# Block attention with routed tokens, heavy half: another order of the steps on TensorE and ScalarE

## The reference

```python
light_out = light_local_attn(x, ...)      # windows of 128 tokens, 8 heads of 64
scores_q, idx_q = route(x, q_routing_token, 256)     # 256 of the tokens as queries
scores_kv, idx_kv = route(x, kv_routing_token, 512)  # all 512 tokens as keys
routed_out = heavy_attn(routed_q, routed_kv, scores_kv, ...)
heavy_out = zeros.at[idx_q].set(routed_out * scores_q)
return light_out + heavy_out
```

```python
q = (rmsnorm(xq) @ wq)          # 256 queries, 8 heads of 64
k, v = (rmsnorm(context) @ wkv) # 512 keys, 8 heads of 64
out = softmax(q k^T) v @ wo
```

## Time and profile before

| | us |
|---|---|
| median of three runs | 2500.14 |
| the profiled execution, its own time | 2494.2 |
| its span | 2492.2 |
| PE busy in the span | 2329.9 (93%) |
| DVE / ACT / POOL busy | 1410.5 / 950.6 / 613.6 |
| heavy half (first scores of step 0 to the last product with values) | 575.96 to 974.6 |

### The profile page before, as it was taken

The page is one execution under the profiler, slowest core; times in us unless marked ns, Lnnn a source line. Parts: engine busy times, 40 slices in busy tenths (PEclk is TensorE's granted clock), DMA queues, the critical chain, the costliest instruction groups (busy, mean ns, idle before and its releaser), DMA issues.

```text
span 2492.2 us, 40543 instructions
## 1 busy us (share of the span) xinstructions
PE 2329.9 (93%) x15438; PEld 1656.4 (66%) x15438; DVE 1410.5 (57%) x2881; ACT 950.6 (38%) x2288; POOL 613.6 (25%) x548
## 2 busy tenths in 40 slices
PE   6997999999999998998999999988984999999998
PEld 4444677776666665444666665544553999999997
DVE  7886654674544555887466533348885444444442
ACT  1366655444444543332233322124653222222222
POOL 3234222252001002211233100014455122222222
PEclk8998999999999999999999999989996999999999
DMA  5011211121001000100001029502126222222221
GB/s 202 1 35 51 91 35 52 52 83 54 26 26 52 26 26 26 71 1 18 1 1 36 1 95 326 185 0 110 40 80 244 58 36 37 35 36 36 36 35 26
DMA packets 72087, 148.36 MB, mean 60 GB/s; under 512 B 11704, under 2 KB 59065, under 8 KB 69441
## 3 DMA queue, kind: packets, MB, share of 16 engines
q1 hardware_dynamic: 39600, 104.61, 12.3%
q0 software_dynamic: 16368, 26.23, 5.4%
q10 hardware_dynamic: 15936, 15.03, 2.1%
HBM read 107.42 MB, written 74.76 MB: 73 GB/s over the span
## 4 chain that ended last, share of the span: by engine, by line
PE 81%; DVE 10%; ACT 4%; issue 2%; POOL 2%; DMA 1%; SPq 0%; DVEq 0%; POOLq 0%; ACTq 0%
PE PS L2366 14%; PE PS L2392 7%; PE PS L2822 5%; PE PS L2834 5%; PE PS L1540 4%; PE PS L1531 4%; PE PS L2050 3%; PE PS L2062 3%; PE PS L2891 3%; PE PS L602 3%; PE PS L2882 3%; PE PS L2856 3%; DVE mem L1148 2%; DVE mem L1143 2%; PE PS L2927 2%
## 5 line engine op out<-in xcount | busy, mean ns | idle before, releaser
L2366 PEld LDWEIGHTS PS<-ctx2T,x_all 128*128 128x128 f32 x3124 | 361.2, 193 | 10.1 <-DVE x_all L2515 6.5
L2366 PE MATMUL PS<-ctx2T,x_all 128*128 128x128 f32 x3124 | 361.8, 276 | 5.9 <-DVE x_all L2515 5.1
L2563 POOL DMA_INDIRECT out_x<-xnT,moe_small x71 | 130.9, 1843 | 427.7 <-ACT xnT L2448 424.7
L2392 PE MATMUL PS<-mem,moe_small 128*128 x852 | 195.8, 379 | 0.8 <-ACT xnT L2448 0.8
L2515 DVE COPY x_all<-mem 128x2816 f32 x71 | 115.5, 1627 | 109.6 <-issue 96.9
L2392 PEld LDWEIGHTS PS<-mem,moe_small 128*128 128x128 f32 x852 | 156.4, 190 | 19.4 <-issue 1.2
L1148 DVE RECIPROCAL mem<-PS 128x512 f32<-128x512 f32 x48 | 160.9, 3351 | 11.3 <-PE PS L671 11.0
L1143 DVE TENSOR_REDUCE mem<-PS 128x32 f32<-128x2048 f32 x48 | 109.9, 2289 | 50.8 <-PE PS L627 50.7
L3208 DVE TENSOR_REDUCE moe_small<-PS 128x2 f32<-128x1024 f32 x64 | 78.5, 1226 | 99.2 <-PE PS L2882 99.2
L3353 POOL TENSOR_TENSOR mem<-mem,moe_small 128x512 f32<-128x512 f32 x64 | 82.2, 1304 | 207.5 <-DVE moe_small L3218 207.4
L3032 ACT ACTIVATE mem<-PS,moe_small 128x128 f32<-128x128 f32 x256 | 89.9, 377 | 94.2 <-DVE moe_small L3203 94.2
(11 more groups left out here) (382 smaller groups left out, 4596.9 us busy)
## 6 DMA issues: line engine op xcount, KB each, us to landing
slots<-in_trash_rows SPq DMA_DIRECT2D x8, 4290.0 KB, 63.8
mem<-in_L_ffn_experts SPq DMA_DIRECT2D x8, 2176.0 KB, 13.6
xn<-slots ACTq DMA_DIRECT2D x53, 130.0 KB, 2.1
x_all<-in_x SPq DMA_DIRECT2D x8, 512.0 KB, 8.1
xn<-unit_rows SPq DMA_DIRECT2D x8, 512.0 KB, 4.5
mem<-unit_rows SPq DMA_DIRECT2D x8, 512.0 KB, 4.3
out_x<-x_all ACTq DMA_DIRECT2D x8, 512.0 KB, 2.9
unit_rows<-moe_small SPq DMA_DIRECT2D x7, 512.0 KB, 3.2
```

Of the source, the lines that this page charges most:

```text
L2366: last = nc.tensor.matmul(PS[:, moe_bank(j, part), c * P:(c + 1) * P], m.w[:, j % 2, k, at:at + P], m.rowT[:, j % 2, k, :], start=k == 0, ...
L2392: last = nc.tensor.matmul(PS[:, MOE_BANK_Y, 0:D], m.hT[:, j % 2, n, :], w[:, :, at:at + D], start=n == 0, stop=n == KE - 1)
L2563: nc.gpsimd.indirect_dma_start(s.T["out"], bass.IndirectOffsetOnAxis(s.token[:, j % 4:j % 4 + 1], 0), m.result[:, j % 4, :], None, compute ...
```

## The change

The change only moves calls. On PE, `heavy_values(u - 1)` at the end of step u becomes `heavy_values(u - 2)` directly behind the scores of step u (`light_values` of the last two light steps likewise), and the last one falls into a step 65. In odd steps `queries` moves in front of `turn_probs`. `turn_routed` moves from the odd step into the even step in front of it, to its end. ACT is put in the matching order: in odd steps it first copies the finished pair of products (`copy_heavy_oT`, before in the even step), then the queries, then does the exponentials, then copies the two turned halves; before, it copied the halves, did the exponentials and then copied the queries. DVE and POOL are unchanged, and no instruction is added or removed.

```diff
--- before.py
+++ after.py
@@ -2970,22 +2970,20 @@
         nxt = u // QT + 1
         if u < HEAVY_STEPS:
             heavy_scores(u)
-        if u == 0:
-            light_values(LIGHT_STEPS - 2)
+        if u < 2:
+            light_values(LIGHT_STEPS - 2 + u)
+        elif u <= HEAVY_STEPS + 1:
+            heavy_values(u - 2)
         if u % QT == 0 and nxt < LIGHT_STEPS:
             keys(heavy, nxt)
-        if u % QT == 1 and nxt < LIGHT_STEPS and nxt % CT == 0:
-            turn_routed(nxt // CT)
+        if u % QT == 1 and nxt < LIGHT_STEPS:
+            queries(heavy, nxt)
         if u <= HEAVY_STEPS:
             turn_probs(*((heavy, u - 1) if u else (light, LIGHT_STEPS - 1)))
         if u % QT == 0 and nxt < LIGHT_STEPS:
             values_of_tokens(heavy, nxt)
-        if u % QT == 1 and nxt < LIGHT_STEPS:
-            queries(heavy, nxt)
-        if u == 0:
-            light_values(LIGHT_STEPS - 1)
-        elif u <= HEAVY_STEPS:
-            heavy_values(u - 1)
+            if nxt % CT == 0:
+                turn_routed(nxt // CT)
         if LIGHT_STEPS + u - Y_LATER < NT:
             light_out(LIGHT_STEPS + u - Y_LATER)
         i, qt = (u - 2 * CT - 1) // (2 * CT), (u - 2 * CT - 1) % (2 * CT)
@@ -3092,25 +3090,23 @@
             nc.scalar.activation(s.e_min[0:B, :], s.e[0:B, :], ACT.Exp).then_inc(s.sems["score_row"], 1)
     for u in range(HEAVY_STEPS + 3):
         nxt = u // QT + 1
-        if u % QT == 1 and nxt < LIGHT_STEPS and nxt % CT == 0:
-            copy_routed(nxt // CT)
+        if u % QT == 1 and 2 <= u <= HEAVY_STEPS + 1:
+            copy_heavy_oT(u // QT - 1)
+        if u % QT == 1 and nxt < LIGHT_STEPS:
+            copy_queries(heavy, nxt)
+        if u < HEAVY_STEPS:
+            heavy_exponentials(u)
+        if u < 2:
+            copy_light_oT(LIGHT_STEPS - 2 + u)
         if u % QT == 1 and u <= HEAVY_STEPS:
             copy_probs(heavy, u - 1, 0)
             copy_probs(heavy, u - 1, 1)
-        if u < HEAVY_STEPS:
-            heavy_exponentials(u)
-        if u == 0:
-            copy_light_oT(LIGHT_STEPS - 2)
         if u % QT == 0 and u <= HEAVY_STEPS:
             copy_probs(*((heavy, u - 1) if u else (light, LIGHT_STEPS - 1)), 0)
         if u % QT == 0 and nxt < LIGHT_STEPS:
             copy_values(heavy, nxt)
-        if u % QT == 1 and nxt < LIGHT_STEPS:
-            copy_queries(heavy, nxt)
-        if u == 0:
-            copy_light_oT(LIGHT_STEPS - 1)
-        elif u <= HEAVY_STEPS and u % QT == 0:
-            copy_heavy_oT(u // QT - 1)
+            if nxt % CT == 0:
+                copy_routed(nxt // CT)
         i, qt = (u - 2 * CT - 1) // (2 * CT), (u - 2 * CT - 1) % (2 * CT)
         if u > 2 * CT and qt < QT:
             act.wait_ge(heavy.sems["y_psum"], QT * i + qt + 1)
```

## The result

The changed kernel takes 2513.2 us (median of 19 runs, 2505.77 to 2515.88), the kernel before 2503.39 us (19 runs, 2499.08 to 2506.93). The ratio is 1.0034, with a 95% interval from 1.0026 to 1.0042: slower by 0.34%, between 6.5 and 10.5 us, where 7.8 had been worked out. In itself the median lies 5.3 us above the 2507.9 of the forecast; 3.3 of these are its base, since the three runs it started from had a median of 2500.14 and the 19 have 2503.39.

A forecast was written before the change was run, and what follows sets the result against it. TensorE, busy 373.6 of 384 us between 576 and 960, was taken as the bound. Odd steps +9.9, start -1.0 and +1.5, end -2.6 gave +7.8; 2500.1 + 7.8 = 2507.9 us, range 2497 to 2514.

The forecast's parts named there:

- The odd step: Heavy odd steps with queries, without output product: exponentials wait for the queries' copy, 0.45 longer each, 22 times, +9.9 us.
- the bound of 0.55: Upper growth per odd step, if the exponentials wait for the copy's full 0.40: +12.1 us in all.
- The even step: Heavy even steps: same groups, routed queries' turning only moves here, next scores at 6.65; costed at nothing.
- the cover of 0.1: Even step: copies for the product with values ready at 5.96, wanted at 6.06, leaving 0.1 us.
- The steps with an output product: Nine odd steps: output product of 1.92 carries TensorE's work to 5.89, past 5.00, so nothing changes.
- 2.5 us either way: Transposes cost 0.87 behind keys, 0.93 behind scores: 0.06 either way in 42 steps, 2.5 at most.
- span of +5 to +12: Range of the forecast's own case for the whole change, in us; that case was given 74%.
- The start: First heavy steps: one product leaves, -1.0 us; one wait before step 1's light output product, +1.5.
- The end: Scores of step 62 to next stage: 12.85 us with one product more, instead of 15.43, so -2.6.
- The faster one: Odd steps: the queries' copy does not hold the exponentials, all 22 waits go, -14.9 us, 2485; 8%.
- The wait did not stay as it was: Rival for odd steps: the wait stays as long, only the two ends count, -2.1 us, 2498; 14%.
- The clock: Rival: the clock falls behind each of the 22 waits, +33 us on top, 2541; 4%.

The follow-up runs named there:

- e1: Changed kernel with ScalarE alone reordered in odd steps, exponentials ahead of the copy of the queries: 2494.66 us, ratio 0.9959 to the kernel before.
- e6: Changed kernel with each heavy copy of the queries made twice on ScalarE in odd steps: ratio 1.0064 to the kernel before.
- e4: Kernel before, with each step's output product moved ahead of its last product with values, step 1 excepted: ratio 0.9985.
- the second executions: Kernel before and changed kernel, each profiled once more unchanged: heavy half 398.6 and 406.1 us.
- e3: Changed kernel with the queries back behind the transposes on TensorE, and copied after the exponentials on ScalarE: 2524.25 us, ratio 1.0073 to the kernel before.
- e2: Changed kernel with queries directly behind odd scores, products with values behind queries or keys, ScalarE copying queries first: 2501.67 us, ratio 0.9996 to the kernel before.
- e5: Changed kernel with products with values at the step's end, queries directly behind odd scores, heavy output products one step later: 2491.84 us, ratio 0.9946 to before.
- e9: Kernel with products at the step's end and queries behind odd scores, without the heavy half's gathers (work left out): 2474.6 us, ratio 0.9922 to before.

## Why the prediction was right

**The odd step** was the largest term, and its mechanism held: the copy of the queries stands ahead of the exponentials, the exponentials hold the score banks, and the wait grows (e1 takes it away, e6 lengthens it, the count of 22 is exact). The term was under-sized: 0.45 a step was worked out and 0.56 measured (5.11 against 4.55). With the seven turnings of routed queries, which cost 0.49 in an odd step before and 0.44 in an even one now, that is 12.2 us instead of 9.9. Of the missing 0.11, 0.10 is that the queries' matmuls end 1.13 behind their start in the new place, not 1.03. The rest is that TensorE went on 0.14 behind the exponentials and not 0.10, less 0.02 or 0.03 in how long the copy holds ScalarE. It ended a little past the bound of 0.55, which had been drawn from another reason, the copy's full length: the copy holds ScalarE for 0.28 (716.97 to 717.25), not for its 0.38.

**The even step** held: 6.66, and no product with values waits for its copies in spite of the cover of 0.1. The copies ended (718.57 + 1.09) 0.83 behind the next scores, and the product started at 1.06.

**The steps with an output product** are the term that the prediction missed. It costed them at nothing ("nothing changes"). Its 2.5 us either way were for the transposes' new neighbours only, and its span of +5 to +12 does not hold even these. Measured: 0.15 in each odd and 0.20 in each even one, 17 of them from step 2 on, together 3.0 us less. e4 shows it without the rest of the change.

**The start** was put at +1.5 less one product of 1.02, that is +0.5: measured +0.4 (575.46 to 591.39 is 15.93, 575.96 to 591.46 was 15.50). **The end** was put at -2.6: measured -2.4. But 1.6 of this is the clock, which fell in the end of the kernel before in the one execution and not in the other. Against the second executions the end is 0.8 shorter and the first two steps are 0.8 shorter too (16.08 against 16.89). The forecast had taken both from one trace, and neither is a fixed price.

Measured terms: +12.2, +0.4, -3.0, -2.4, together +7.2, to 0.1 us the heavy half's difference; in the second executions +12.2, -0.8, -3.0, -0.8, together +7.6, where the halves differ by 7.5. What repeats is the +12.2 and the -3.0. The path and the largest term of the forecast were right, but that +7.8 came so close was luck: two errors of 2.3 and 3.0 us cancelled. The medians of 19 runs differ by 9.8 and their interval reaches from 6.5 to 10.5, so 7.3 is inside it; whether the other 2.5 us are the change's stays open, since the stages behind scatter by more than that. The line between slower and unchanged, 0.3%, was passed by 0.04%, and the interval reaches below it.

**The rivals.** The faster one (the copy does not hold the exponentials) needed the queries copied by 2.41. In the change their copy starts at 3.25, and it fell. e1 shows the point of decision to have been real: once the exponentials do not wait for the copy, they start at 2.49. It reaches odd steps of 4.30, though, not the 3.97 of the rival, and 9.6 us under the median before, not 14.9. The wait did not stay as it was. The clock, at 1.00 in 576 to 960, did not fall there, although the waits doubled. The page "TensorE: Matmul & The Clock Gate" of the Trainium skill, section "A second HAM failure mode: psum-queue depth-cycling", has short idle spells swing the clock. No run here shows that with 22 waits of 1.03 or of 1.5 (e3): the granted clock is 1.00 from 576 to 960 in both.

## What to carry to other kernels

When a step is moved forward on the busy engine, work out the moment at which each engine that frees a buffer for it can start, and look at the order on that engine too: here the copy that TensorE had been waiting for was taken ahead of the exponentials that TensorE had to wait for anyway, and the wait doubled. A releaser named in a table of waits is only the last one; the one behind it was 0.27 us away, so at most half of the wait could be had by moving the copy alone. And a term that is read off one execution, as the end of the half was here, can be that execution's: a second trace of the same kernel tells. A group of matmuls has no fixed price either: what stands beside it counts, and over the 17 steps with an output product that came to 3.0 us, against 7.3 for the whole change.

## What the runs showed of the hardware

**Neighbours on TensorE.** A group of 8 matmuls of 256 columns with full 128 x 128 loads costs 1.82 us behind a group with full loads and 1.92 behind a product with values (128 x 64 loads). The queries' results are there after 1.13 instead of 1.03 where they stand behind a product or behind scores. Scores (64 x 128 loads) and products side by side cost 2.08 together whichever stands first; with keys between them the even step is 0.15 longer (6.81 in e2 against 6.66). That the two groups with half-size loads do best side by side was not expected. The Trainium skill, page "TensorEngine Tiling (Array Packing)", section "Key Properties", says that a change of the tiling mode drains TensorE, with no price. The rows agree in that a group costs more behind one with loads of another shape; but scores behind products change the shape too and show no such price, so not every change costs the same.

**The clock behind a wait.** The same wait left the clock full in one execution and not in another. Behind the wait of 2.26 us in step 62 the product was recorded at 1.62 us in the first execution of the kernel before and at 1.97 in e4, but at 1.09 in the second execution of the kernel before. Behind the wait of 1.82 in step 63 it took 1.09 in both executions of the changed kernel, and 1.64 and 1.76 in e1 and e6. In e3 the product behind a wait of 1.33, later in the end, took 1.72. So the length of the last wait alone does not decide; what does, these runs do not tell.

**VectorE beside GpSimd's indirect transfers.** In the odd steps of e5 where the maxima are late they start 1.34 to 1.49 us behind the scores (five steps) and 2.96 (one), where 1.18 is usual; the steps are 0.10 to 0.25 us longer, and the one 1.7. Without the gathers none is late (e9). In both kernels, in e1 and in e2 there are as many gathers, and no maxima of an odd step from step 3 on are late. Nothing hides it there: in e1 the exponentials start 0.08 behind the end of the maxima (700.58 against 699.27 + 1.23) and would show a late start. The gathers lie elsewhere: there they begin in the odd step with an output product and go on in the even one behind it, whose maxima are on time, while in e5, which has its output products one step later, the last of the four is issued at 5.9 to 6.1 us of the even step ahead or in the odd step itself. In the next stage of the changed kernel's first profile a maximum of VectorE started 1.24 us late beside the same kind of gather, in the second executions of both kernels 0.5 late, and at once in the first profile of the kernel before; this is one place where two executions of one program part by up to a microsecond. What in the two engines meets there, no run tells. The page "GPSIMD Engine Reference" of the Trainium skill, section "Key points", has GpSimd contend with VectorE's instructions that have two inputs in SBUF or run in a mode with two ports; the maxima have one input, and it is in PSUM (PS), and they start late all the same.
